# First stage of a two-layer FFN kernel: activations and first weights on one load queue, the first conversion split, eight warm-up matmuls

## What is computed

```
def _L0_cond_ref(x, language_ids, W, Wr, A, B):
    base = jnp.einsum('btd,od->bto', x, W)
    logits = jnp.einsum('btd,ed->bte', ...x, ...Wr)
    # bias on one expert per sequence, top 2 of 8, softmax -> gates
    h = jnp.einsum('btd,erd->bter', x, A)
    lora_out = jnp.einsum('bter,bte,eor->bto', h, gates, B)
    return base + SCALING * lora_out

x = x + _L0_ffn_ref(_L0_cond_ref(x, ...), ...)      # 4-bit weights: dequantise, gate and up, silu, down
x = x + _L1_ffn_ref(_L1_cond_ref(x, ...), ...)      # weight chosen per sequence, RMS norm, gate and up, silu, down
```

## Time and profile before

| | |
|---|---|
| median of three runs | 446.32 us (446.04 to 447.08) |
| profiled execution, its own time | 446.06 us |
| its span, first to last instruction | 444.3 us |
| mean granted TensorE clock | 0.999 |
| TensorE busy (PE) | 439.1 us, 99% of the span |
| weight loads (PEld) | 358.6 us, 81% |
| VectorE (DVE) | 341.6 us, 77% |
| ScalarE (ACT) | 219.4 us, 49% |
| POOL | 188.9 us, 43% |
| DMA | 79.96 MB, mean 180 GB/s |

### The profile page before, as it was taken

One profiled execution on the slowest core, in us unless ns is written; L12 is line 12 of the kernel. 1 busy time (PEld: TensorE's weight loads), 2 busy tenths in 40 slices (PEclk: granted clock), 3 DMA queues, 4 the chain that ended last, 5 costly groups with the idle time before them and its releaser, 6 DMA issues.

```text
span 444.3 us, 5507 instructions
## 1 busy us (share of the span) xinstructions
PE 439.1 (99%) x1946; PEld 358.6 (81%) x1946; DVE 341.6 (77%) x439; ACT 219.4 (49%) x283; POOL 188.9 (43%) x167
## 2 busy tenths in 40 slices
PE   8999999999999999999999999999999999999997
PEld 4688888888888888888888778888888888888885
DVE  4689997788777978948778567868688678999922
ACT  5415755666542213347677656466466554474200
POOL 2077887855008201900005778886997300000000
PEclk9999999999999999999999999999999999999999
DMA  8765133100008694386279517947668146986623
GB/s 292 182 210 162 44 105 107 49 1 1 1 4 276 191 352 204 131 327 252 97 260 333 211 47 238 287 166 217 226 212 273 63 137 261 351 288 177 231 90 142
DMA packets 30344, 79.96 MB, mean 180 GB/s; under 512 B 2497, under 2 KB 15585, under 8 KB 28657
## 3 DMA queue, kind: packets, MB, share of 16 engines
q1 hardware_dynamic: 26464, 68.04, 45.0%
q0 software_dynamic: 3280, 10.83, 7.8%
q10 hardware_dynamic: 576, 0.80, 0.6%
HBM read 58.95 MB, written 20.72 MB: 179 GB/s over the span
## 4 chain that ended last, share of the span: by engine, by line
PE 98%; DMA 1%; ACT 0%; DVE 0%; issue 0%
PE ps L1890 10%; PE ps L1892 10%; PE ps L1891 10%; PE ps L1635 10%; PE ps L1639 10%; PE ps L1636 10%; PE ps L1994 5%; PE ps L1992 5%; PE ps L1752 5%; PE ps L1750 5%; PE ps L1751 5%; PE ps L1993 5%; PE ps L1873 2%; PE ps L1871 2%; PE ps L1872 2%; DMA res<-in_xT 1%
## 5 line engine op out<-in xcount | busy, mean ns | idle before, releaser
L1635 PE MATMUL ps<-h_hi,ring_hi 128*128 128x512 f32 x152 | 59.1, 389 | 0.0
L1636 PE MATMUL ps<-h_lo,ring_hi 128*128 128x512 f32 x152 | 59.1, 389 | 0.0
L1088 DVE TENSOR_TENSOR ring_lo<-raw,ring_hi 128x1792 fp32r<-128x1792 f32 (+1 forms) x23 | 47.6, 2073 | 14.7 <-ACT ring_hi L725 14.7
L1890 PE MATMUL ps<-zt_hi,ring_hi 128*128 128x512 f32 x140 | 54.5, 390 | 0.4 <-issue 0.4
L1892 PE MATMUL ps<-zt_hi,ring_lo 128*128 128x512 f32 x140 | 54.5, 389 | 0.0
L1891 PE MATMUL ps<-zt_lo,ring_hi 128*128 128x512 f32 x140 | 54.5, 389 | 0.0
L1639 PE MATMUL ps<-h_hi,ring_lo 128*128 128x512 f32 x152 | 47.8, 389 | 0.0
L725 ACT ACTIVATE ring_hi<-raw 128x1792 fp32r<-128x1792 f32 (+1 forms) x23 | 36.7, 1594 | 22.3 <-PE ps L1892 10.1
L1636 PEld LDWEIGHTS ps<-h_lo,ring_hi 128*128 128x128 f32 x152 | 28.5, 188 | 6.0
L1635 PEld LDWEIGHTS ps<-h_hi,ring_hi 128*128 128x128 f32 x152 | 28.5, 188 | 5.9
L1639 PEld LDWEIGHTS ps<-h_hi,ring_lo 128*128 128x128 f32 x152 | 28.5, 188 | 5.9
(11 more groups left out here) (252 smaller groups left out, 1115.3 us busy)
## 6 DMA issues: line engine op xcount, KB each, us to landing
ad_raw<-in_w1T SPq DMA_DIRECT2D x8, 1024.0 KB, 6.3
wd<-down_weights SPq DMA_DIRECT2D x7, 1024.0 KB, 5.5
down_weights<-dhi SPq DMA_DIRECT2D x7, 896.0 KB, 4.4
down_weights<-dlo SPq DMA_DIRECT2D x7, 896.0 KB, 4.3
raw<-in_gu SPq DMA_DIRECT2D x12, 512.0 KB, 3.7
wd<-down_weights SPq DMA_DIRECT2D x7, 768.0 KB, 5.1
draw<-in_d SPq DMA_DIRECT2D x7, 512.0 KB, 5.4
dn_work<-in_qw_dn SPq DMA_DIRECT2D x11, 256.0 KB, 4.7
```

The source lines that it names most:

```text
L1088: dve.tensor_tensor(dst, src, hi_part.bitcast(F32), ALU.subtract).then_inc(done_sem, 1)
L1635: pe.matmul(ps[:, bank + hf, :], w_hi, v_hi[:, t], start=first, stop=False)
L1636: pe.matmul(ps[:, bank + hf, :], w_hi, v_lo[:, t], start=False, stop=False)
L1890: pe.matmul(ps[:, bank, :], ring1_hi[s][:, w], z_hi[:, t], start=first and k == 0, stop=False, skip_group_check=True)
```

## The change

The four loads of `aw_raw` go from ScalarE's queue to SP's, each ahead of or behind an x load in the order of use. The conversion of the first block of weights is made in two instructions, 128 and 256 columns, so the semaphore `s_whi0` counts one more, and all later waits on it are raised by one. TensorE's first matmul of each half waits for the first of the two parts, the second and third for both. There are eight warm-up matmuls in place of ten.

```
         @block.sync
+            def load_aw(k):
+                c = slice(3 * P * k + KD * E * (k > 0), 3 * P * (k + 1) + KD * E)
+                sp.dma_start(aw_raw[:, c], a["aw"][:, c]).then_inc(s_aw[k], 16)
+
             load_x(0)
+            load_aw(0)
             load_x(1)
-            for i in range(2, len(X_PIECES)):
-                load_x(i)
+            for k in range(1, KD):
+                load_x(k + 1)
+                load_aw(k)
             sp.dma_start(w0b_raw[:, :, :], a["w0b"]).then_inc(s_w0b, 16)
...
         @block.scalar
-            def aw_cols(k):
-                return slice(3 * P * k + KD * E * (k > 0), 3 * P * (k + 1) + KD * E)
-
-            for k in range(KD):
-                act.dma_start(aw_raw[:, aw_cols(k)], a["aw"][:, aw_cols(k)]).then_inc(s_aw[k], 16)
-
...
             def aw_hi_part(k):
                 act.wait_ge(s_aw[k], 16)
-                hi(aw_hi[:, k, :], aw_piece(k), s_whi0)
+                if k:
+                    hi(aw_hi[:, k, :], aw_piece(k), s_whi0)
+                else:
+                    hi(aw_hi[:, 0, 0:P], aw_piece(0)[:, 0:P], s_whi0)
+                    hi(aw_hi[:, 0, P:3 * P], aw_piece(0)[:, P:3 * P], s_whi0)
...
         @block.vector
             def aw_lo_part(k):
-                dve.wait_ge(s_whi0, k + 1)
+                dve.wait_ge(s_whi0, k + 2)
...
-            dve.wait_ge(s_whi0, KD + 1)
+            dve.wait_ge(s_whi0, KD + 2)
...
-            dve.wait_ge(s_whi0, KD + 2)
+            dve.wait_ge(s_whi0, KD + 3)
...
         @block.tensor
             pe.wait_ge(s_warm, 1)
-            for _ in range(10):
+            for _ in range(8):
                 pe.matmul(ps[:, 0, :], warm[:, 0:P], warm, start=True, stop=True)
...
                 pe.wait_ge(s_xhi, hf + 1)
-                pe.wait_ge(s_whi0, 1)
                 for j, bank in enumerate((6, 0, 4)):
+                    pe.wait_ge(s_whi0, min(j, 1) + 1)
                     pe.matmul(ps[:, bank + hf, :], aw_hi[:, 0, P * j:P * j + P], act_hi[:, 0, th], start=True, stop=False)
```

## The result

The changed kernel took 446.9 us (median of 20 executions, 445.75 to 450.38), the kernel before 445.98 on the same chip (20 executions, 445.53 to 447.08). The medians differ by 0.9 us. The ratio of the executions is 1.0026, with a 95% interval of 1.0016 to 1.0037: slower by 0.26%, about 1.2 us. The forecast was 445.7, between no visible difference and a gain. The profiled execution took 447.22 us, 445.4 of them span, against 444.3 before.

A forecast was written before the change was run, and what follows sets the result against it. TensorE, busy 439.1 of 444.3 us, was taken as the bound. The profiled 446.06 less a 0.56 us lead gave 445.5, or 445.76 from the median of 446.32; predicted 445.7, range 445.0 to 446.5.

The forecast's parts named there:

- Start of the product: TensorE's first real matmul was to start at about 4.95 us, 1.06 sooner than 6.01.
- The split conversion: ScalarE's first weights in 128 and 256 columns: 0.30 and 0.40 us, together 0.19 more than before.
- The 0.4 to 0.6 us left for stragglers: First loads: allowance for slow DMA engines beyond volume, so x lands at about 3.75 us, the weights at 4.5.
- If the clock rises at 6.35 as before: First products: real matmuls from 4.95 to 6.35 us run at 0.43 each, leaving a lead of 0.56 us, not 1.06.
- rival B: First products: clock rises before real work, whole lead arrives; gain 1.06 to 1.36 us, time 445.0 to 445.3; chance 0.24.
- one queue brings it in the order of use, so no later than now: x block 3: low part ready at 13.70 us, first used at 15.81, no later with one queue.
- the queue then holds megabytes that haven't moved, so nothing starves: SP's queue: four more issues of some 0.45 us each ahead of w0b, b, pz and nib do no harm.
- Rival E: Loads of x and weights: one queue carries less than two; stall of 3.2 us at x block 3, 449.0 us; chance 0.04.
- the slack at the gates: VectorE's product with the gates, 30.93 to 32.16 us, matmul behind at 33.49: 1.3 us slack against a lead of 0.6 to 1.1.
- The removal gives nothing by itself: Start of TensorE: eight warm-ups end at 4.65 us and clear the way for the product at 4.95; ten would end at 5.5.
- D: Gap behind eight warm-ups with late loads: clock's rise begins anew, 12 matmuls slower, 2.4 us, time 448.6; chance 0.03.

The follow-up runs named there:

- the queue alone: Kernel before with only the change's loads, all on SP's queue, ten warm-ups, one conversion: 447.4 us, 0.9973; repeated 447.25 us, 1.0036.
- the kernel with one block behind six activations: Changed kernel with nine warm-ups and the weights of k = 1 issued by ScalarE behind six one-column activations: 447.0 us, 0.9993 against the kernel before.

## Why the prediction was wrong

**Start of the product: right.** x's high part begins at 3.93 (3.75 forecast for the landing), the weights landed at 4.5 as forecast, the product started at 4.96 against 4.95. The split conversion took 0.62 us against the 0.70 summed. The 0.4 to 0.6 us left for stragglers fitted these first loads.

**The clock: not as forecast, in our favour.** "If the clock rises at 6.35 as before" failed. Three products took 0.78 us from 4.96 to 5.74, and the first router matmul came 1.10 us sooner, not 0.56: rival B as far as that point. The moment of the rise isn't fixed. The ten warm-ups of the queue alone took 3.94 us in one profile and 4.45 in the other. The Trainium skill, TensorE: Matmul & The Clock Gate, Part 1, lets it move by about 500 ns; by the spacings here it lay anywhere from about 4.2 us (the kernel with one block behind six activations, whose last two warm-ups start 0.25 us apart) to 6.35 (before), which is more.

**The failed step: "one queue brings it in the order of use, so no later than now".** With it fell "the queue then holds megabytes that haven't moved, so nothing starves". A full queue was taken for a full rate, and for loads whose parts arrive together. x block 3 landed at 12.35 us and not at 11.07, its weights at 13.06 and not at 9.99, and its low part, counted on by 13.70, was ready at 15.82, only 0.4 us ahead of its use; w0b, whose landing the prediction does not time, came at 16.30 and not at 12.29. Rival E had the lower rate, with a chance of 0.04, and its evidence against was one row, 0.41 MB in the microsecond from 10 to 11. The row is right, but it is of a program whose second queue had carried a share until the microsecond before. DMA queues of the kernel before, 9 to 10 us:

```profile
q1 hardware_dynamic: 103, 0.39, 94.9%
q10 hardware_dynamic: 38, 0.04, 10.2%
```

In the change, with one queue from the beginning, the same microsecond from 10 to 11 moves 345 GB/s and not 414. The row did not carry over to the other program. The Trainium skill, DMA: Bandwidth & Descriptors, Issuing engines are not separate DMA queues, says that a second issuing engine saves only the time of issuing. The runs speak against it for this stretch: 262 to 334 GB/s from one queue over 6 to 9 us, 398 to 415 where ScalarE began by 1.2 us to issue 576 KB or more.

E's price was off too, and no rival had the spread of the parts: E left 0.6 us for stragglers, where the last part of w0b came 3.5 us behind its ninth. It foresaw one stall of 3.2 us at x block 3. Measured are four small ones (0.62, about 0.1, 0.36 and 0.24 us, with their refills and late steps), which took the lead from 1.10 to -1.1 us, 2.2 in all. Its threshold of 290 GB/s was too low, since it looked at x block 3 alone: at 334 the weights of k = 1 and the loads behind x (w0b, b) were already late.

**The second step that failed: the slack at the gates.** "VectorE waits for a gather of zeros, which comes by DMA and doesn't move with TensorE", with 1.3 us of slack. True, but it moves with the load queue: zeros are unpacked on VectorE behind b's low part, the gather starts at 24.36 and not 21.95 us, and VectorE's product at 33.19 and not 30.93. The slack of 1.3 us was counted against an earlier TensorE and not against a later gather. The prediction named 30 to 33 us as the place where misread slack would show, and it did, at 34.

**Warm-ups: half right.** "The removal gives nothing by itself" was too kind. Alone it costs 0.22%, because it opens a gap of 0.94 us before the clock has risen. D's mechanism was right and its chance too small for a kernel with that gap; in the change the early start closes the gap. Whether some of its 20 executions (up to 450.38) paid for it, its two profiles cannot show.

## What to carry to other kernels

When loads are merged onto one queue, the sum has to carry a rate, and a spread between a load's first and last part, measured with one queue alone over the same stretch; a load is as late as its last part. And every load behind them has to be followed to its last consumer, not only those that are reordered. Look for the in-order engine that has a late load ahead of unrelated work: here b's conversion held the logits on ScalarE and the zeros on VectorE. Warm-ups should reach the first real product; two too many cost nothing here, two too few cost some 1.8 us in 8 of 12 executions.

## What the runs showed of the hardware

- With all loads on one hardware queue, 262 to 334 GB/s moved over 6 to 9 us at a DMA share of 0.81 to 0.98; with 576 KB or more on a second one whose issues began by 1.2 us, 398 to 415, and in one of these kernels the first queue alone then moved 0.83 MB from 7 to 9 us.
- With one queue the sixteen parts of w0b (512 KB) landed over 3.6 to 4.8 us (six profiles), with a second one filled early over 0.5 to 0.6 us (seven profiles; 1.6 in an eighth).
- A DMA issue on ScalarE came at 1.19 us, ahead of the activation before it in the program, which began at 2.05.
- A load issued at 4.56 us on a second, empty queue moved its first packet at 8.95 us; one issued at 0.75 us moved its first at 1.8.
- A gap of 0.79 to 1.03 us behind eight warm-ups that took 3.59 us or more, all at the lower level, was followed by 0.43 us a matmul until 9.4 to 9.8 us (four kernels). The same gap behind warm-ups that had taken 3.52 us, the last one quicker, was not. Nor was one of 1.26 us behind ten that had taken 4.01. Gaps of 0.18 to 0.38 us never were.
- Idle times of TensorE of 2.5, 2.8, 3.1 and 3.2 us in the middle of full work were each followed by a granted clock of 0.50 to 0.55, so such a stall costs more than itself.
- In two kernels VectorE stood 2.40 and 3.98 us before its product with the gates with all named inputs there. What held it stays open.
